# Three Vector operations in another order, and the second sequence's mapped product one step earlier

## What is computed

```python
# attention: 16 heads of 8 channels, each query sees a window of 64 keys
q, k, v = x @ Wq.T, x @ Wk.T, x @ Wv.T          # split into heads
p = softmax(where(mask, q @ k.T / sqrt(8), -1e30))
out = (p @ v) @ Wo.T
# ffn: 16 experts of width 64, 4 of them chosen per token by a sigmoid gate
# in 4 groups, and a shared expert of width 128
inter = silu(x @ w_gate[e]) * (x @ w_up[e])
y = sum_e combine[token, e] * (inter @ w_down[e])
y = y + (silu(x @ sw_gate) * (x @ sw_up)) @ sw_down
```

## Time and profile before

| | us |
|---|---|
| median of 3 runs (lowest, highest) | 715.27 (715.05, 715.5) |
| the profiled execution | 716.24 |
| its span in the profile | 714.4 |
| TensorE matmuls busy | 659.0 |
| VectorE busy | 588.1 |
| ScalarE busy | 525.8 |
| GpSimd busy | 495.6 |

### The profile page before, as it was taken

The page is one execution under the profiler, slowest core; times in us unless marked ns, Lnnn a source line. Parts: engine busy times, 40 slices in busy tenths (PEclk is TensorE's granted clock), DMA queues, the critical chain, the costliest instruction groups (busy, mean ns, idle before and its releaser), DMA issues.

```text
span 714.4 us, 19501 instructions
## 1 busy us (share of the span) xinstructions
PE 659.0 (92%) x6232; PEld 521.2 (73%) x6232; DVE 588.1 (82%) x1710; ACT 525.8 (74%) x1603; POOL 495.6 (69%) x635
## 2 busy tenths in 40 slices
PE   3989889999999999999999999999999999989997
PEld 2877767777777777777777777777777777777875
DVE  3687888888889897889889897988979888897663
ACT  3786778697878878787887878787887878764332
POOL 4413367778778787878778777777878777876523
PEclk9999999999999999999999999999999999999999
DMA  5010032230403132140413123040322214040321
GB/s 173 1 32 30 2 101 66 59 123 11 141 29 119 59 105 73 40 138 2 142 34 119 59 76 102 2 147 29 119 59 96 82 32 119 15 135 33 118 77 45
DMA packets 50245, 52.60 MB, mean 74 GB/s; under 512 B 5664, under 2 KB 31904, under 8 KB 50080
## 3 DMA queue, kind: packets, MB, share of 16 engines
q1 hardware_dynamic: 50208, 52.14, 23.6%
HBM read 43.20 MB, written 4.72 MB: 67 GB/s over the span
## 4 chain that ended last, share of the span: by engine, by line
PE 42%; DVE 24%; ACT 19%; issue 10%; POOL 2%; DVEq 1%; DMA 1%; ACTq 0%; POOLq 0%; SPq 0%
ACT probs L626 9%; PE PS L1077 6%; PE PS L933 6%; DVE neg_max L809 6%; PE PS L895 5%; PE PS L1024 5%; PE PS L897 5%; PE PS L896 5%; ACT q_by_head L581 5%; DVE tu L798 4%; DVE probsT L765 3%; PE PS L1047 3%; DVE sums L775 3%; PE PS L963 2%; ACT k_by_row L581 2%
## 5 line engine op out<-in xcount | busy, mean ns | idle before, releaser
L626 ACT ACTIVATE probs<-PS,neg_max 128x96 f32<-128x96 f32 (+1 forms) x1024 | 246.8, 350 | 87.7 <-DVE neg_max L809 87.5
L504 POOL TENSOR_TENSOR gate<-gate,spread 128x512 f32<-128x512 f32 x124 | 158.1, 1275 | 96.6 <-ACT gate L581 40.8
L509 POOL TENSOR_TENSOR hh<-gate,tu 128x512 f32<-128x512 f32 x108 | 138.7, 1284 | 19.3 <-DVE tu L798 12.8
L809 DVE TENSOR_REDUCE neg_max<-PS 128x4 f32<-128x384 f32 (+1 forms) x256 | 121.6, 513 | 25.5 <-PE PS L933 25.0
L1077 PE MATMUL PS<-wd,hh 128*128 128x128 f32 x1024 | 137.9, 278 | 3.5 <-DVE hh L865 1.7
L1077 PEld LDWEIGHTS PS<-wd,hh 128*128 128x128 f32 x1024 | 126.5, 192 | 12.2 <-issue 4.3
L798 DVE SCALAR_TENSOR_TENSOR tu<-th,PS 128x512 f32<-128x512 f32 x128 | 87.4, 683 | 48.5 <-ACT th L597 36.6
L895 PE MATMUL PS<-x_hi,w_hi 128*128 128x512 f32 x288 | 125.0, 434 | 0.0
L897 PE MATMUL PS<-x_lo,w_hi 128*128 128x512 f32 x288 | 114.7, 398 | 0.0
L765 DVE STREAM_TRANSPOSE probsT<-probs 128x768 f32<-128x768 f32 (+1 forms) x128 | 114.4, 894 | 0.0
L896 PE MATMUL PS<-x_hi,w_lo 128*128 128x512 f32 x288 | 114.0, 396 | 0.0
(11 more groups left out here) (107 smaller groups left out, 991.3 us busy)
## 6 DMA issues: line engine op xcount, KB each, us to landing
spread<-weights_by_expert SPq DMA_DIRECT2D x248, 128.0 KB, 3.0
X<-x SPq DMA_DIRECT2D x32, 256.0 KB, 3.6
OUT<-H SPq DMA_DIRECT2D x16, 256.0 KB, 3.0
out<-OUT SPq DMA_DIRECT2D x16, 256.0 KB, 3.8
ffn_stage<-w_gu SPq DMA_DIRECT2D x1, 1152.0 KB, 6.7
wd<-w_down SPq DMA_DIRECT2D x1, 512.0 KB, 6.8
weights_by_expert<-cT SPq DMA_DIRECT2D x16, 32.0 KB, 1.6
probsT<-w_att SPq DMA_DIRECT2D x1, 192.0 KB, 3.1
```

Source lines behind the costliest of these rows:

```text
L504: tt(gate2[:, :], gate[:, k % 2, :], spread[:, k % SP_BUFS, :], ALU.mult).then_inc(s_g2, 1)
L509: tt(hh[:, k % 2, :], gate2[:, :], tu[:, k % 2, :], ALU.mult).then_inc(s_h, 1)
L626: ins = nc.scalar.activation(probs[:, u % PROB_BUFS, tt, 2 * rows + e, j0:KW], PS[:, rows, n * KW + j0:n * KW + KW], ACT.Exp, bias=neg_max ...
L809: v_.tensor_reduce(neg_max[:, rows, :], src[:, :, j0:KW], AX_X, ALU.max, negate=True).then_inc(s_m, 1)
```

## The change

The mapped product of the second sequence becomes stage 18 in place of 19, so step 2 in place of 3 (`OT = (15, 18)`); `either` finds which of the two falls on a step, and the waits that named `OT + 4` name `OT[1]`. The order of uses of the two banks is the same, with OT at step 2 in front of XT2. On VectorE the division becomes a function, `divide`, which is called right behind the maxima; in the steps of `MAXIMA_FIRST` that is ahead of the take. Step 7 joins `MAXIMA_FIRST`. As divisions fall on steps 2 and 7 alone, both steps now have the order maxima, division, take. ScalarE's, GpSimd's and SyncE's orders stay, but for the places that name OT.

```diff
--- before.py
+++ after.py
@@ -50,7 +50,7 @@
 SUMS = (11, 12, 13, 13, 14, 14, 15, 16)
 TURN = (14, 16)
 EXPAND = (15, 17)
-OT, OW = 15, 16
+OT, OW = (15, 18), 16
 LN2 = 17
 XT2 = 19
 LG = 24
@@ -69,7 +69,7 @@
 EARLY, POST, LATE, WEIGHTS = range(4)
 USES = sorted([(stage % STEPS, place, stage) for place, stages in (
     (EARLY, (VP, LG)), (LATE, (XT, QP, KP, XT2, XT2 + 4, SH)),
-    (POST, (OT, OT + 4, OW, OW + 4, SH)), (WEIGHTS, (CT,)))
+    (POST, (*OT, OW, OW + 4, SH)), (WEIGHTS, (CT,)))
     for stage in stages])
 assert len({use[:2] for use in USES}) == len(USES)
 SPLIT = ((LATE, XT),)
@@ -91,6 +91,15 @@
             if slot.fixed and not 0 <= slot.n - off < NG:
                 return None, 0
             return Group(slot.n - off, (slot.par + off) % 2, slot.fixed), k
+    return None, 0
+
+
+def either(slot, s, stages):
+
+    for b, stage in enumerate(stages):
+        g, _ = at(slot, s, stage)
+        if g:
+            return g, b
     return None, 0
 
 
@@ -174,7 +183,7 @@
 LOADS, FFN_LOADS = 4, 6
 PREPARE = 4
 BUSY = 8
-MAXIMA_FIRST = (2, 3)
+MAXIMA_FIRST = (2, 3, 7)
 ORDER_PER_SLOT = 5
 ROUTING_DVE, ROUTING_POOL = 8, 5
 NO_SCORE, GROUP_IN = -3.0e38, 2.0 ** 60
@@ -476,7 +485,7 @@
                         g, _ = at(sl, s, stage)
                         if g:
                             if not (g.fixed and g.n == 0):
-                                taken(pool, slot_before(sl), (OT + 4 * b) % STEPS, POST)
+                                taken(pool, slot_before(sl), OT[b] % STEPS, POST)
                             pool.wait_ge(s_sum_t, g.n * GB + b + 1)
                             whole = [P, NQ, Q]
                             tt(by_block[:, b, :, :], sums_t[:, b, :].unsqueeze(1).broadcast_to(whole),
@@ -808,8 +817,19 @@
                             src = PS[:, rows, 0:4 * KW].rearrange("p (n k) -> p n k", n=4)
                             v_.tensor_reduce(neg_max[:, rows, :], src[:, :, j0:KW],
                                              AX_X, ALU.max, negate=True).then_inc(s_m, 1)
+                    def divide():
+                        g, b = either(sl, s, OT)
+                        if g:
+                            side, bank = filled(dve, sl, s, POST)
+
+                            dve.wait_ge(s_o, g.n * GB + b + 1)
+                            v_.tensor_tensor(oT[:, :], o_f[:, :], bank[:, 0:T], ALU.mult).then_inc(s_taken[side], 1)
+
                     if s in MAXIMA_FIRST:
+                        divide()
                         take_up()
+                    else:
+                        divide()
                     g, _ = at(sl, s, HS)
                     if g:
                         fill = SH % STEPS
@@ -825,12 +845,6 @@
                         taken(dve, sl, (OW + 4 * b) % STEPS, POST)
                         stats(sl, H2[:, g.par, 2 * b:2 * b + 2, :], 2, st2, mv2).then_inc(s_mv2, 1)
 
-                    g, b = at(sl, s, OT, 4, GB)
-                    if g:
-                        side, bank = filled(dve, sl, s, POST)
-
-                        dve.wait_ge(s_o, g.n * GB + b + 1)
-                        v_.tensor_tensor(oT[:, :], o_f[:, :], bank[:, 0:T], ALU.mult).then_inc(s_taken[side], 1)
                     g, b = at(sl, s, OW, 4, GB)
                     if g:
                         side, bank = filled(dve, sl, s, POST)
@@ -1015,7 +1029,7 @@
                         if turn_ == 0:
                             pe.wait_ge(s_vb, g.n + 1)
                         if not later and not (g.fixed and g.n == 0 and b == 0):
-                            taken(pe, slot_before(sl) if b else sl, (OT if b else OT + 4) % STEPS, POST)
+                            taken(pe, slot_before(sl) if b else sl, OT[1 - b] % STEPS, POST)
                         pe.wait_ge(s_pt, g.n * NU + 4 * b + (4 if later else 3))
                         for kb in range(4 * later, 4 * later + 4):
                             nq = min(3, NQ - kb)
@@ -1039,7 +1053,7 @@
                     g, b = at(sl, s, OW, 4, GB)
                     if g:
                         side, bank = free(POST)
-                        taken(pe, sl if b else slot_before(sl), (OT + 4 * b) % STEPS, POST)
+                        taken(pe, sl if b else slot_before(sl), OT[b] % STEPS, POST)
                         if g.fixed and g.n == 0 and b == 0:
                             pe.wait_ge(s_wf, 16 * FFN_LOADS)
                         for half in range(2):
```

## The result

The changed kernel takes 691.11 us (median of 4 runs, 690.29 to 691.27) against 715.38 us of the kernel before beside it: ratio 0.966, 95% interval 0.964 to 0.967. The profiled execution took 691.06 us with a span of 689.3, so between the two profiled executions lie 25.2 us.

The account below looks back on a forecast made before the run. TensorE, busy 92%, was taken as the bound, waiting for the division to free shared PSUM banks. 13 slots x 1.39 = 18.1 us plus 0.6 in the fill gave 18.7 off, median 696.6 us; range 693.5 to 706.

Parts of the forecast that it names:

- Step 7: VectorE's maxima and division ahead of the take start step 0's logits 1.01 us earlier; the later take costs nothing.
- Survival through steps 0 to 2: The whole 1.01 us reaches step 2's maxima; step 0's mask matmul clears ScalarE's exponentials by 0.5 us.
- Rival 1: Mask matmuls of step 0 or 1 meet ScalarE's exponentials, only 0.19 us passes there: 707.3 us; chance 0.10.
- The tie of step 2: TensorE's loads and VectorE's take both allow step 3's gate matmuls at 331.13, 0.69 us earlier, without cover.
- Step 3: Product and division leave; ScalarE's copy of the routing weights loses its 0.38 us wait, giving 1.39 us a slot.
- the fill: Pipeline start: the product leaves step 3's path in two slots, 0.30 us each, 0.6 us gained.
- Rival 4: TensorE's path, not ScalarE's, leads and VectorE's idle 0.41 us in step 7 helps: 1.6 us a slot, 693.9; chance 0.07.
- the long slot: One full-pipeline slot of 42.21 us against 40.78, at clock 0.96; its 1.4 us excess was called not the kernel's order.

Follow-up runs that it names:

- the order alone: Kernel before with only VectorE's order changed (maxima, division, take in steps 7 and 3), mapped product kept at stage 19: 693.21 us, ratio 0.970.

## Why the prediction was wrong in size

- **Step 7: right, 0.09 us short.** 1.01 forecast, 1.10 measured. The division and the take followed at the distances taken from the rows (0.92 and 0.33 for 0.94 and 0.32). The Trainium skill, page "VectorE: DVE Perf Modes", section "The DRAIN you can't avoid", says that a next operation waits for the emptied pipe, and adds that one that is not held starts earlier. The first would have given 0.41 for the second distance; the trace shows the second case, as the row of the kernel before did.
- **Survival through steps 0 to 2: right in the gain, in part by luck.** Rival 1 (ScalarE) did not come; the mask matmul of step 0 waits for issue only. The tie of step 2 held (0.67 for 0.69), and two experiments show that it is a tie: 0.23 us a slot lost for 0.33 put in, nothing won by taking the take out of the way. But the 0.67 is two errors that cancel: 1.12 us arrived where 1.01 was carried, and the mapped product cost 0.45 where its two loads had been carried at 0.32 (the down product's loads behind it, at 319.22, took 1.08 us in place of 0.97).
- **Step 3: the term that failed.** 0.38 us, read from ScalarE's printed idle time, was 0.52; and the copy of the second input came 1.16 earlier where 1.01 was carried. Together with step 7: 1.69 for 1.39, 3.2 us over twelve slots. The path was right, as the mask matmul of step 4 still waits for the exponentials (0.43); the size was not. The bounds of a slot, 1.1 to 1.5, came from the ties alone and left out the error of the reading itself. With 1.66 in 13 slots the forecast's own sum gives 693.1, just under the range; the fill, 1.5 us more than forecast, takes the result further below.
- **Rival 4** came nearest in size, 1.6 us a slot, but its cause, that TensorE's path leads, is not what the trace shows in step 3.
- **The clock: the second failure.** The prediction set the long slot apart as "not the kernel's order" and wrote that a second one might come and "none takes as much off". It belonged to the kernel's order: it sat behind the very wait that the change removes, and such slots came back with the wait. It is 1.5 us between the profiled executions; against the medians about 1 of it had been taken off already. In the fill 1.1 us more are clock, whose cause stays open.
- **The fill**: 0.6 + 1.01 forecast, 3.2 measured, of which 1.1 clock; 0.3 of the rest is there before the first changed operation (maxima at 50.36 for 50.70), so it is a difference of the start and not the change's.
- **What the change is made of.** Both parts were credited; the order alone brings 21.5 of the 24 us.

## What to carry to other kernels

Cost a removed wait by the distance between the starts of the two operations before and after, against the same distance where nothing waits; the printed idle time is short by the overlap of queued operations, and on a periodic path the error is multiplied. A stretch of half clock that stands behind a wait may belong to that wait: put the wait back and see, and price it with the wait. Before crediting a two-part change, ask of each wait whether either part alone would end it.

## What was not expected of the hardware

- Behind one pause of TensorE's loads of 1.23 to 1.26 us, followed by eight matmuls of 16 columns, the upper clock was lost for about 3 us, 1.5 us of time, in up to 5 of the loop's 12 slots; a pause of 0.6 to 0.7 us before the same matmuls cost nothing in four runs (clock 0.999 to 1.000).
- Operations in ScalarE's queue start 0.15 us before the recorded end of the one ahead (0.89 apart, 1.04 long), and in VectorE's 0.08 (0.33 apart, 0.41 long).
